# A graph layer kernel on one core: the product with W_r in a third gather stage, one stored row per node instead of two

## The chip, the core and the metric

The kernel runs on one core of one Trainium2 chip. A core has TensorE (PE, matrix products into PSUM), VectorE (DVE), ScalarE (ACT), GpSimd (POOL, which here issues the indirect DMAs) and SyncE (SP, which issues the plain DMAs); they run side by side and wait for each other by semaphores. The time is that of one execution on the device in microseconds (us), the median of several runs: 2688.31 us for the kernel before, from three runs between 2688.16 and 2688.74.

## The reference

There are 12500 nodes with 256 features (D) and 200000 edges, sorted by destination. With xn the normalised x, the reference computes

```python
agg = _mean_aggregate(xn, edge_index, N)           # mean of xn[src] over each node's incoming edges
gnn = relu(agg @ W_l.T + b_l + xn @ W_r.T) + xn
# mix: linear attention with 8 heads, then a two-layer MLP, each with a layer norm
Q, K = elu(xn @ Wq) + 1, elu(xn @ Wk) + 1
msg = _layernorm(attention(Q, K, xn @ Wv) @ Wm, g1, b1)
mix = xn + _layernorm(relu(concat([xn, msg]) @ W1) @ W2, g2, b2)
x = x + gnn + mix
# ffn: a router picks the 6249 tokens of largest weight
xf = _layernorm(x)
weights = xf @ wr + br
y = (gelu(xf[sel] @ w1 + b1) @ w2 + b2) * weights[sel]
x = x + xf + scatter(y)
```

## The kernel before

Nodes are padded to 98 blocks of 128 and are handled two blocks at a time, in 49 steps. After a first part that normalises x, writes it as a table `xtab` of node rows (two halves in 16 bits) and sorts out the edges' block numbers, come these stages:

- **Key steps** (49, `k_body`): keys, values and queries of two blocks; the transposed rows go to `xt_d`, the queries to `q_d`.
- **Message steps** (49, `m_body`): query times key sums, product with Wm, norm, the MLP with W1 (`m_hidden`) and W2 (`m_mlp_out`), one step late, norm; the result with the terms of xn goes to `r_d`.
- **Gathers**, beside both: the edges are cut in 392 groups of 512. GpSimd gathers four times 128 source rows per group (line 631) into a ring of six slots and waits for a free slot (`grp_used`). DVE makes a one-hot of the destinations for each block that a group touches (line 778), in a ring of four; TensorE adds the rows up with eight products of one-hot and rows (lines 1365 and 1367, function `seg`), and DVE adds the sum of a finished block into `agg` (line 788, `add_before`). A key step holds two groups, a message step six; in the code of TensorE and DVE each `seg` stands between the products of its step, and this written order is the order of the work.
- **Node steps** (49, `g_body`): ACT scales the sums to means (line 1243), TensorE transposes them (1350), ACT copies them back (1250), TensorE adds the products with W_r and W_l (1517), DVE adds b_l (963), applies relu and adds the row of `r_d` (966), takes the statistics of the norm (852 to 860); ACT writes the normalised row and the row of the result (1276), both of which SP stores to `ff_d` and, the second, to `out`; DVE takes the dot product with wr (950) for the token weight (955).
- **Choice of tokens**: eight rounds of counting (1003, PE 1535), then ranks and the list of chosen nodes.
- **Feed-forward steps** (25 of up to 256 tokens, `f_body`): GpSimd gathers rows of `ff_d` (line 654) and scatters results (664); TensorE makes each product of single-precision numbers from three of split halves (1576), 96 matmuls a step; ACT applies gelu, DVE makes the low halves (1085), the token weights and the results.

`steps(eng, body, n, unroll)` writes the first `unroll` steps out, puts the middle ones in a loop of `unroll` steps per pass, and writes the last out; where the number is Python's, code is straight.

Of the kernel before, what the change touches and what calls it, by code (L numbers as in the profile page):

```python
# [5 lines left out]
f32 = mybir.dt.float32  # L6
# [16 lines left out]
KG, MG = 2, 6  # L23
NG = NSUP * (KG + MG)
# [31 lines left out]
assert 0 < LASTC < P and KG * 3 == RING and MG == RING  # L56
# [43 lines left out]
def build(nc, x, src, dst, W_l, b_l, W_r, Wq, Wk, Wv, Wm, W1, W2, g1, b1, g2, b2, wr, br, w1, fb1, w2, fb2, out):  # L100
# [13 lines left out]
    with ctx:  # L114
# [12 lines left out]
        ff_d = nc.dram_tensor("ff_d", (NPAD, 2 * D), f32, kind="Internal").ap()  # L127
# [42 lines left out]
        fb2_s = sb("fb2_s", [P, D])  # L170
        wr_s = sb("wr_s", [P, D])
# [43 lines left out]
        G_T = (BA, BD)  # L215

# [6 lines left out]
        wts_in = sem("wts_in")  # L223
        wlr_in = sem("wlr_in")
# [75 lines left out]
        g_in = [sem(f"g_in{i}") for i in range(4)]  # L300
# [5 lines left out]
        g_v = sem("g_v")  # L306
        g_base = sem("g_base")
        g_w = sem("g_w")
        ff_out = [sem(f"ff_out{i}") for i in range(2)]
# [13 lines left out]
        f_xT_h = sem("f_xT_h")  # L323
        f_xT = sem("f_xT")
# [5 lines left out]
        f_w = sem("f_w")  # L330
# [36 lines left out]
        gxT = [w1_s[:, s, :].rearrange("p (a b) -> p a b", a=2) for s in range(4)]  # L367
        gma = [part(work, 2048 + 512 * s, (2, D)) for s in range(2)]
        gaT = [part(work, 3072 + 512 * s, (2, SB)) for s in range(2)]
        gx1 = [part(work, 4096 + 512 * s, (2, D)) for s in range(2)]  # L370
        gff = [part(work, 5120 + 1024 * s, (2, 2 * D)) for s in range(2)]
        gs = onehot[:, :, :, :].rearrange("p k t m -> p (k t m)").bitcast(f32)[:, 0:2 * D].rearrange("p (a b) -> p a b", a=2)
# [15 lines left out]
        s_blk = topk[:, 1200:1200 + NSEL]  # L388
# [6 lines left out]
        sel_idx = pool2[:, 1168:1168 + NSEL].bitcast(i32)  # L395
# [3 lines left out]
        fstg = [pool2[:, 1760 + 2 * k:1762 + 2 * k].bitcast(i32) for k in range(FSLOTS)]  # L399
# [31 lines left out]
        def m_place(i, t):  # L431

            g = KG * NSUP + t
            return g % RING, g // RING + i
# [10 lines left out]
                       (fb2_s[:, :], fb2.unsqueeze(0).to_broadcast([P, D])),  # L445
                       (wr_s[:, :], wr.rearrange("d o -> o d").to_broadcast([P, D])),
# [3 lines left out]
                       (fb1_s[:, :], fb1.rearrange("(c p) -> p c", p=P))]  # L450

# [8 lines left out]
        def _(e):  # L460
# [83 lines left out]
            for i in (NSUP - 2, NSUP - 1):  # L544
                e.wait_ge(m_r, i + 1)
                e.dma_start(rows(r_d, 2 * i), mr[i % 2]).then_inc(r_out[i % 2], 16)
            for s in range(2):
                e.wait_ge(r_out[s], 16 * len(range(s, NSUP, 2)))
# [1086 lines left out]
```

## Time and profile before

| | |
|---|---|
| median of three runs | 2688.31 us |
| profiled execution: time, span | 2688.11 us, 2686.4 us |
| PE busy | 2269.3 us (84%) |
| PE weight loads | 1880.8 us (70%) |
| DVE busy | 1324.9 us (49%) |
| ACT busy | 958.1 us (36%) |
| POOL busy | 1617.3 us (60%), of it line 631 1478.2 |
| granted TensorE clock, mean | 0.913 of full speed |
| chain that ended last | PE 35%, POOL 33% (line 631 32%), issue 14%, DVE 12% |
| DMA | 412.28 MB, mean 153 GB/s |

The span reaches from the first to the last instruction; the time also holds what lies around it, 1.7 us here. Busy shares are averages over stages with different limits, so they say little about a single stage. PE's matmuls overlap, so what a product costs is better read from the starts of neighbours. A row of the order of time gives the start and the duration in us, the engine, the line, the operation, what it writes and reads, and how many of a kind follow each other; in brackets the idle time ahead of it and what ended it.

### The profile page before, as it was taken

Reading aid. Unit: us, or ns where it says so; the run is one execution under the profiler, and the core shown is the slowest. Engines: PE = TensorE matmul, PEld = TensorE weight load, DVE = VectorE, ACT = ScalarE, POOL = GpSimd, SP = SyncE. Lnnn points to the kernel's source line nnn. Section 1 sums busy time; section 2 is a strip of 40 time slices with the busy share of each in tenths; the row PEclk is TensorE's granted clock in tenths of the full one; section 3 lists DMA queues with packets and bytes.
Section 4 is the critical chain, followed back from the end, with each engine's and each line's share of the span. In section 5 each row is a group of like instructions: output and inputs, shape, how many; then the busy total and the mean of one; then the engine's idle time right before and its main releaser. Section 6 shows DMA issues by size and latency. Waiting matters only on the chain.

```text
span 2686.4 us, 50791 instructions
## 1 busy us (share of the span) xinstructions
PE 2269.3 (84%) x13646; PEld 1880.8 (70%) x13647; DVE 1324.9 (49%) x3290; ACT 958.1 (36%) x2185; POOL 1617.3 (60%) x1719
## 2 busy tenths in 40 slices
PE   1299999988988898888888888888888999379998
PEld 1287777766776776676767776676766777269998
DVE  7644444443334334443444444545454788854444
ACT  7433333321222222222222222222222899235544
POOL 2577777777777777777777777777774000023332
PEclk7599999998888889989988999999999999579999
DMA  9766666664444444444444444444442899212221
GB/s 313 219 196 190 184 186 182 181 187 138 140 138 142 139 140 137 144 140 140 137 143 140 136 140 142 142 138 138 137 144 86 275 312 311 92 48 67 66 66 42
DMA packets 229947, 412.28 MB, mean 153 GB/s; under 512 B 38193, under 2 KB 129715, under 8 KB 229886
## 3 DMA queue, kind: packets, MB, share of 16 engines
q0 software_dynamic: 81296, 224.22, 29.2%
q1 hardware_dynamic: 147774, 186.59, 20.9%
q10 hardware_dynamic: 816, 0.79, 0.1%
q8 instruction: 22, 0.36, 0.1%
q14 instruction: 39, 0.32, 0.0%
HBM read 315.13 MB, written 96.32 MB: 153 GB/s over the span
## 4 chain that ended last, share of the span: by engine, by line
PE 35%; POOL 33%; issue 14%; DVE 12%; DMA 3%; ACT 1%; DVEq 1%; POOLq 0%
POOL gath_raw L631 32%; PE ps L1576 11%; PE ps L1410 5%; PE ps L1442 4%; PE ps L1365 4%; PE ps L1367 3%; DMA gath_raw<-xtab,srcI 2%; PE ps L1424 2%; DVE work L966 1%; DVE onehot L963 1%; PE ps L1452 1%; DVE onehot L950 1%; PE ps L1350 1%; PE ps L1484 1%; PE ps L1465 1%
## 5 line engine op out<-in xcount | busy, mean ns | idle before, releaser
L631 POOL DMA_INDIRECT gath_raw<-xtab,srcI x1563 | 1478.2, 946 | 476.4 <-issue 461.5
L1365 PE MATMUL ps<-gath_raw,onehot 128*128 128x256 f16 x1956 | 495.5, 289 | 197.8 <-DMA gath_raw<-xtab,srcI 106.7
L1367 PE MATMUL ps<-gath_raw,onehot 128*128 128x257 f16 x1956 | 497.7, 290 | 0.0
L778 DVE SCALAR_TENSOR_TENSOR onehot<-ps,blkbase,dstF 128x512 f32 x489 | 353.3, 746 | 262.2 <-issue 175.1
L1442 PE MATMUL ps<-work,w_s 128*128 128x256 f32 x1568 | 403.2, 415 | 0.7
L1365 PEld LDWEIGHTS ps<-gath_raw,onehot 128*128 x1956 | 199.7, 102 | 287.7 <-issue 254.0
L1442 PEld LDWEIGHTS ps<-work,w_s 128*128 128x128 f32 x1568 | 319.2, 209 | 49.5 <-issue 0.5
L852 DVE BATCH_NORM_STATS2 stats<-ps 128x6 f32<-128x256 f32 x196 | 74.4, 422 | 490.3 <-PE ps L1484 480.1
L1576 PE MATMUL ps<-split_raw 128*128 128x256 f32 x2376 | 292.7, 285 | 1.7 <-DVE split_raw L1076 1.5
L1576 PEld LDWEIGHTS ps<-split_raw 128*128 128x128 f32 x2376 | 287.8, 192 | 2.4 <-issue 1.9
L1193 ACT ACTIVATE work<-ps 128x512 f32<-128x512 f32 x98 | 58.5, 597 | 643.5 <-PE ps L1442 643.5
L1367 PEld LDWEIGHTS ps<-gath_raw,onehot 128*128 x1956 | 200.9, 103 | 43.7
L643 POOL COPY agg<-agg 128x2 int32 (+2 forms) x25 | 6.7, 268 | 347.3 <-DVE agg L1065 309.3
L1410 PE MATMUL ps<-wkv_s,work 128*128 128x256 f32 x784 | 183.8, 388 | 5.0 <-issue 4.2
L1452 PE MATMUL ps<-w_s,work 128*128 128x256 f32 x784 | 182.1, 385 | 1.0 <-ACT work L1193 0.7
L1410 PEld LDWEIGHTS ps<-wkv_s,work 128*128 128x128 f32 x784 | 146.6, 192 | 25.0 <-issue 4.8
L1452 PEld LDWEIGHTS ps<-w_s,work 128*128 128x128 f32 x784 | 145.0, 190 | 20.0 <-ACT work L1193 1.1
L1350 PE MATMUL ps<-ident,work 128*128 128x128 f32 x784 | 126.9, 285 | 16.1 <-ACT work L1243 15.7
L1310 ACT ACTIVATE agg<-ps,fb_s 128x256 f32<-128x256 f32 x200 | 83.9, 470 | 137.8 <-PE ps L1576 137.7
L664 POOL DMA_INDIRECT out_rows<-agg x49 | 48.5, 990 | 135.7 <-DVE agg L1105 123.7
L1198 ACT ACTIVATE small<-small 128x2 f32<-128x2 f32 x98 | 19.8, 203 | 303.4 <-DVE small L860 303.1
L1465 PE MATMUL ps<-kvbd,work 128*128 128x128 f32 x392 | 111.3, 379 | 14.5 <-issue 9.8
(204 smaller groups left out, 3157.4 us busy)
## 6 DMA issues: line engine op xcount, KB each, us to landing
work<-x_in SPq DMA_DIRECT2D x98, 256.0 KB, 3.7
ff_d<-work SPq DMA_DIRECT2D x49, 512.0 KB, 2.8
gath_raw<-xtab,srcI POOLq DMA_INDIRECT x1563
agg<-x_in SPq DMA_DIRECT2D x14, 896.0 KB, 7.2
xtab<-gath_raw SPq DMA_DIRECT2D x14, 896.0 KB, 4.9
xt_d<-work SPq DMA_DIRECT2D x49, 256.0 KB, 4.1
q_d<-work SPq DMA_DIRECT2D x49, 256.0 KB, 2.4
work<-q_d SPq DMA_DIRECT2D x49, 256.0 KB, 3.3
```

What stands on the lines that cost most here:

```text
L631: e.indirect_dma_start(out=gath[:, TPG * s + t, 0:2 * D], out_offset=None, in_=xtab[:, :], in_offset=bass.IndirectOffsetOnAxis(ap=srcI[:, ...
L778: v.scalar_tensor_tensor(out=onehots[:, ds(p % OHN * TPG, TPG), :], in0=ps[:, columns:columns + 1, 0:P].to_broadcast(shape), scalar=blkbas ...
L852: last = v.bn_stats(ln_st[k][:, u, :], src[:, u, :])
L1310: last = a.activation(fh[:, c, :], bank(BB + h)[:, c % 2, :], ACT.Gelu_apprx_tanh, bias=fb1_s[:, c:c + 1])
L1350: last = t.transpose(bank(b)[:, c, u * P:(u + 1) * P], of[:, u, c * P:(c + 1) * P], ident[:, :])
L1365: t.matmul(ps[:, ds(BG + k % 2, 1), 0:D], oh, gath[:, r, 0:D], start=False, stop=False, skip_group_check=True)
L1367: last = t.matmul(ps[:, ds(BG + k % 2, 1), 0:AGW], oh, gath[:, r, D:2 * D + 1], start=False, stop=q == TPG - 1, skip_group_check=True)
L1410: last = t.matmul(bank(BC + b)[:, u, :], kxT[s][:, c, u * P:(u + 1) * P], wkv_s[:, c, b * D:(b + 1) * D], start=c == 0, stop=c == 1)
L1442: last = t.matmul(bank(BD + h)[:, o_ % 2, :], w1_s[:, c, o_ * P:(o_ + 1) * P], (mxT[s] if c < 2 else mynT)[:, c % 2, :], start=c == 0, sto ...
L1452: last = t.matmul(bank(BF)[:, u, :], mh1[:, c, u * P:(u + 1) * P], w2_s[:, c, :], start=c == 0, stop=c == 3)
L1465: t.matmul(bank(BB)[:, u, c * P:(c + 1) * P], q, kvbd[:, c, :], start=True, stop=True)
L1576: last = t.matmul(to, left[l], right[r], start=start and k == 0, stop=stop and k == 2)
```

## The change

The 49 message steps hold five groups instead of six, and a third stage of 49 steps (`l_body`) follows them with one group each. In each of its steps TensorE multiplies the transposed rows of two blocks (loaded again from `xt_d`) with W_r, DVE adds b_l from PSUM to SBUF (`l_even`), and SP stores the 128x512 result to the new `lin_d`. The last message step's MLP products stand in the first two steps of that stage, with their norms on DVE. TensorE's message loop and the new one are written out six times per pass instead of two; each message step begins with a group, ahead of the query product. The ring of one-hots has six entries instead of four.

In the node steps TensorE reads the row of `lin_d` through the identity into PSUM (128x512) and adds the W_l products to it; DVE's one operation from PSUM applies relu and adds `r_d`. Means and variances of all blocks are kept; scale and shift are computed for two steps at a time on four columns. ACT writes only the row of the result. The token weight is computed at the end from the dot product of the row before the norm, its mean and its scale, for all 98 blocks at once. PSUM banks for the sums: four instead of two; buffers of sums: five instead of two; of loads and stores: four. The steps are straight code on all engines.

`ff_d` is gone. Four numbers per node (mean, a factor, the token weight; 16 bytes) go to `coef_d` from DVE's first search round (`coefficients`), and a feed-forward step gathers each token's row from `out` and its numbers from `coef_d`, four gathers instead of two; DVE makes the normalised row from them (`f_norm`, ahead of the transposes), and no longer takes the dot product there. The weight rows `wr_s` and `fb2_s` are loaded after the last group, into the room of the gather ring.

```diff
-KG, MG = 2, 6
-NG = NSUP * (KG + MG)
+KG, MG, LG = 2, 5, 1
+NG = NSUP * (KG + MG + LG)
-OHN = 4
+OHN = 6
+GRING, GXRING, GBANKS = 4, 5, 4
+GCOEF = 4
-        ff_d = nc.dram_tensor("ff_d", (NPAD, 2 * D), f32, kind="Internal").ap()
+        lin_d = nc.dram_tensor("lin_d", (NPAD, D), f32, kind="Internal").ap()
+        coef_d = nc.dram_tensor("coef_d", (NPAD, GCOEF), f32, kind="Internal").ap()
+        GP = (BB, BC, BE, BF)
+        fb2_s, wr_s = (gath_raw[:, 5632 + 256 * k:5632 + 256 * k + D] for k in range(2))
...
# SyncE (the stores of the last two message steps and the loads of the node steps move into l_io)
+            l_load(0, 0)
+            l_load(1, 1)
+            def l_io(i, s, j):
...
+                if isinstance(i, int) and i == NSUP - 3:
...
+                    for k in range(GRING):
+                        g_load(k)
+                if isinstance(i, int) and i == NSUP - 1:
+                    e.wait_ge(grp_used, NG)
...
+                            e.dma_start(to, of).then_inc(wts_g, 16)
+                e.wait_ge(l_ps, i + 1)
+                if not (isinstance(i, int) and i >= NSUP - 2):
+                    l_load(i + 2, s)
+                e.wait_ge(l_ev, i + 1)
+                e.dma_start(rows(lin_d, 2 * i), llin[s]).then_inc(l_out[s], 16)
+            steps(e, l_io, NSUP, 2, 3)
-                e.dma_start(rows(ff_d, 2 * i), gff[s]).then_inc(ff_out[s], 16)
-                e.dma_start(rows(out, 2 * i), gff[s][:, :, D:2 * D]).then_inc(ff_out[s], 16)
+                e.dma_start(rows(out, 2 * i), gbase[i % GRING]).then_inc(base_out[i % GRING], 16)
...
# GpSimd, feed-forward part
-                    e.indirect_dma_start(out=frow[s][:, u, :], out_offset=None, in_=ff_d[:, :],
-                                         in_offset=bass.IndirectOffsetOnAxis(ap=fstg[s][:, u:u + 1], axis=0)
+                    e.indirect_dma_start(out=frow[s][0:r, u, D:2 * D], out_offset=None, in_=out[:, :],
+                                         in_offset=bass.IndirectOffsetOnAxis(ap=fstg[s][0:r, u, 0:1], axis=0)
+                                         ).then_inc(f_in[s], 16)
+                    e.indirect_dma_start(out=fco[s][0:r, u, :], out_offset=None, in_=coef_d[:, :],
+                                         in_offset=bass.IndirectOffsetOnAxis(ap=fstg[s][0:r, u, 1:2], axis=0)
                                          ).then_inc(f_in[s], 16)
...
# VectorE, third stage and node steps
+            def l_even(i, s, j):
+                e.wait_ge(l_ps, i + 1)
+                if past(i, 2):
+                    e.wait_ge(l_out[s], 16 * j)
+                v.tensor_tensor(llin[s], bank(BB + s), bcast(bl_s[:, :], 2), ALU.add).then_inc(l_ev, 1)
+            def l_body(i, s, j):
+                g = (KG + MG) * NSUP + i
+                seg(g, BA, *seg_values(e, mybir.EngineType.DVE, g, 1)[0])
+                if past(i, 1):
+                    l_even(i - 1, 1 - s, j - 1 + s)
...
-                own.link(v.tensor_tensor(gs, bank(BB + s), bcast(bl_s[:, :], 2), ALU.add))
...
+            def g_sum(i):
+                x = gx1[i % GXRING]
...
+                v.scalar_tensor_tensor(out=x, in0=bank(GP[i % GBANKS]), scalar=0.0, in1=gr[i % GRING],
                                        op0=ALU.max, op1=ALU.add).then_inc(g_s, 1)
...
+            def g_scale(q):
+                b = slice(4 * q, min(4 * q + 4, NBLK))
+                own.link(v.tensor_scalar(gve[:, b], gmv[:, b, 1], LN_EPS, None, ALU.add))
+                v.reciprocal(grc[:, b], gve[:, b]).then_inc(g_v, 1)
+            def g_affine(q):
...
+            def g_dot(i):
+                for u in range(2):
+                    last = v.tensor_tensor_reduce(out=gjunk[:, u, :], in0=gx1[i % GXRING][:, u, :], in1=wr_s[:, :], scale=1.0,
...
+            for i in range(NSUP):
+                g_sum(i)
+                if i % 2 or i == NSUP - 1:
+                    g_scale(i // 2)
+                g_dot(i)
+                if i % 2 == 0 and i > 0:
+                    g_affine(i // 2 - 1)
+            g_affine(NSUP // 2)
+            own.link(v.tensor_scalar(gsum, gsum, -1.0, None, ALU.mult))
+            own.link(v.scalar_tensor_tensor(out=gdot, in0=gmv[:, :, 0], scalar=gsum, in1=gdot, op0=ALU.mult, op1=ALU.add))
+            own.link(v.tensor_tensor(gdot, gdot, gf, ALU.mult))
+            own.link(v.tensor_scalar(wtok[:, :], gdot, br_s[:, 0:1], None, ALU.add))
...
+            def f_norm(i, s, j):
+                n = 1 if isinstance(i, int) and i == FSTEPS - 1 else 2
+                e.wait_ge(f_in[s], 64 * j + 32 * n)
+                for u in range(n):
+                    last = v.tensor_scalar(frow[s][:, u, 0:D], frow[s][:, u, D:2 * D], fco[s][:, u, 0:1], fco[s][:, u, 1:2],
+                                           ALU.subtract, ALU.mult)
+                last.then_inc(f_ff, 1)
...
# TensorE
-            def m_body(i, s, j):
-
+            def m_body(i, s6, j6):
+                s, j = s6 % 2, j6 * (RING // 2) + s6 // 2
+                g0 = KG * NSUP + MG * i
+                spans = seg_values(e, mybir.EngineType.PE, g0, 1)
+                seg(*m_place(s6, j6, 0), *spans[0])
                 e.wait_ge(m_q_in[s], 16 * j + 16)
...
-                seg(*m_place(i, 5), *spans[5])
-            steps(e, m_body, NSUP, 2)
-            e.wait_ge(m_ynT, NSUP)
-            for h in range(2):
-                m_hidden(NSUP - 1, (NSUP - 1) % 2, (NSUP - 1) // 2, h)
-            m_mlp_out(NSUP - 1)
+            steps(e, m_body, NSUP, RING)
+            def l_body(i, s6, j6):
+                s, j = s6 % 2, j6 * (RING // 2) + s6 // 2
+                seg(*l_place(s6, j6), *seg_values(e, mybir.EngineType.PE, (KG + MG) * NSUP + i, 1)[0])
+                if isinstance(i, int) and i == 0:
+                    e.wait_ge(m_ynT, NSUP)
+                    for h in range(2):
+                        m_hidden(NSUP - 1, (NSUP - 1) % 2, (NSUP - 1) // 2, h)
+                if isinstance(i, int) and i == 1:
+                    m_mlp_out(NSUP - 1)
...
+                        last = t.matmul(bank(BB + s)[:, u, :], lxT[s][:, c, u * P:(u + 1) * P], wrT[:, c, :],
+                                        start=c == 0, stop=c == 1)
+                last.then_inc(l_ps, 1)
+            steps(e, l_body, NSUP, RING, 2)
...
+                t.matmul(flat(to), ident[:, :], flat(glin[i % GRING]), start=True, stop=False, skip_group_check=True)
+                e.wait_ge(g_aT, i + 1)
+                for u in range(2):
+                    for c in range(2):
+                        last = t.matmul(to[:, u, :], gaT[i % 2][:, c, u * P:(u + 1) * P], wlT[:, c, :],
+                                        start=False, stop=c == 1, skip_group_check=True)
```

The names on the left of an arrow are what is written, on the right what is read. TensorE, between the last group of rows and the first node steps, before; 1442 and 1452 are the MLP of the last message step, 1350 the transposes of the means:

```order
L1376 MATMUL ps<-gath_raw 1x1
L1442 MATMUL ps<-work,w_s 128x256 x16
L1452 MATMUL ps<-w_s,work 128x256 x8
L1350 MATMUL ps<-ident,work 128x128 x8
L1517 MATMUL ps<-wrT,w_s 128x256 x2
L1517 MATMUL ps<-wlT,work 128x256 x2
```

The same place now; 1609 is the product with W_r in the third stage, 1448 are the transposes, 1626 the copy through the identity, 1630 the products with W_l:

```order
L1474 MATMUL ps<-gath_raw 1x1
L1609 MATMUL ps<-wrT,wkv_s 128x256 x4
L1448 MATMUL ps<-ident,work 128x128 x8
L1626 MATMUL ps<-w_s,ident 128x512
L1630 MATMUL ps<-wlT,work 128x256 x4
L1448 MATMUL ps<-ident,work 128x128 x4
```

The 24 MLP products are gone from behind the last group, and a node step has four products and one copy where it had eight products (the two rows of 1517 stand twice in a step).

VectorE in one node step before (`small` and `mv` hold the norm's numbers, `wtok` the token weights):

```order
L963 TENSOR_TENSOR onehot<-ps,bl_s 128x512
L966 SCALAR_TENSOR_TENSOR work<-onehot,work 128x512
L852 BN_STATS stats<-ps 128x6 x2
L856 BN_AGGR mv<-stats 128x2 x2
L858 TENSOR_SCALAR small<-mv 128x2
L859 TENSOR_SCALAR small<-mv 128x2
L860 RECIPROCAL small<-small 128x2
L950 ISA onehot,small<-work,wr_s 128x256
L950 ISA small 128x1
L950 ISA onehot,small<-work,wr_s 128x256
L950 ISA small 128x1
L955 TENSOR_SCALAR wtok<-small,br_s 128x2
```

And now, a step of the kind that also does the scale of two steps; what is kept lies in `gath_raw`:

```order
L1013 SCALAR_TENSOR_TENSOR work<-ps,work 128x512
L1017 BN_STATS stats<-work 128x6 x2
L1020 BN_AGGR gath_raw<-stats 128x2 x2
L1026 TENSOR_SCALAR gath_raw<-gath_raw 128x4
L1027 RECIPROCAL gath_raw<-gath_raw 128x4
L1039 ISA gath_raw<-work,gath_raw 128x256
L1039 ISA gath_raw 128x1
L1039 ISA gath_raw<-work,gath_raw 128x256
L1039 ISA gath_raw 128x1
```

One operation of 512 columns is gone, and the small ones stand once for two steps.

GpSimd in the last step of a pass of the feed-forward loop, before and then now (`out_rows` is the result, `agg` names the buffers there):

```order
L643 COPY agg<-agg 128x2
L654 DMA agg<-ff_d,agg 128x512 x2
L664 DMA out_rows<-agg 12544x256 x2
L71 REGISTER_ALU
L71 COMPARE_AND_BRANCH
```

```order
L693 COPY agg<-agg 128x4
L705 DMA agg<-out_rows,agg 128x256
L708 DMA agg<-coef_d,agg 128x4
L705 DMA agg<-out_rows,agg 128x256
L708 DMA agg<-coef_d,agg 128x4
L718 DMA out_rows<-agg 12544x256 x2
L73 REGISTER_ALU
L73 COMPARE_AND_BRANCH
```

Two gathers per step are added between the copy of the indices and the scatters.

## Rows read from the trace of the kernel before

**Rows 1.** Line 631: durations in ns, first and last start; waits (us, times).
```profile
L631 POOL DMA_INDIRECT gath_raw<-xtab,srcI x1563: 942/946/1147, 101.8 to 2054.8; - x196
  PE ps L1376: 14.9, 49
```

**Rows 2.** Waits of TensorE, 630 to 2060 us: total us, times, longest.
```profile
PE ps L1365 <- DMA gath_raw<-xtab,srcI: 95.7, 57, 3.2
```

**Rows 3.** Order of time, TensorE, message steps: start us, us, instructions.
```profile
1350.14 0.39 PE L1365 MATMUL ps<-gath_raw,onehot 128*128 128x256 f16 x1 [2.81 <-DVE onehot L778]
...
1352.06 5.63 PE L1442 MATMUL ps<-work,w_s 128*128 128x256 f32 x16
...
1437.75 0.53 PE L1465 MATMUL ps<-kvbd,work 128*128 128x128 f32 x2
...
1464.29 0.28 PE L1365 MATMUL ps<-gath_raw,onehot 128*128 128x256 f16 x1 [1.83 <-DMA gath_raw<-xtab,srcI]
...
1465.42 0.78 PE L1465 MATMUL ps<-kvbd,work 128*128 128x128 f32 x2
```

**Rows 4.** Order of time, last gather to first node step, TensorE and DVE.
```profile
2063.31 7.17 PE L1442 MATMUL ps<-work,w_s 128*128 128x256 f32 x32
...
2080.71 0.42 DVE L788 TENSOR_TENSOR agg<-agg,ps  x1 [0.19 <-issue]
...
2083.30 0.77 DVE L924 RECIPROCAL rcnt<-rcnt 128x98 f32<-128x98 f32 x1
...
2084.13 0.06 DVE L932 MEMSET small<- 128x1 f32 x1
...
2092.09 0.69 DVE L963 TENSOR_TENSOR onehot<-ps,bl_s 128x512 f32<-128x512 f32 x1 [6.93 <-PE ps L1517]
```

**Rows 5.** Busy us in one stretch: PE, PEld, DVE, ACT, POOL, clock, DMA share, GB/s.
```profile
2090.00:2297.00 207.00, 196.59 (x966) 162.15 (x964) 178.41 (x677) 192.44 (x524) 0.00 (x0) 0.99 0.86 295
```

**Rows 6.** Order of time, DVE, one node step.
```profile
2180.68 0.69 DVE L966 SCALAR_TENSOR_TENSOR work<-onehot,work 128x512 f32<-128x512 f32 x1
2181.40 0.75 DVE L852 BATCH_NORM_STATS2 stats<-work 128x6 f32<-128x256 f32 x2
2182.31 0.25 DVE L856 BATCH_NORM_AGGREGATE mv<-stats 128x2 f32<-128x6 f32 x2 [0.15 <-DVE stats L852]
2182.59 0.17 DVE L858 TENSOR_SCALAR small<-mv 128x2 f32<-128x2 f32 x1
...
2182.98 0.42 DVE L950 CUSTOM_DVE_ANT_0 onehot<-work,wr_s 128x256 f32<-128x256 f32 x1
...
2183.91 0.23 DVE L955 TENSOR_SCALAR wtok<-small,br_s 128x2 f32 x1 [0.15 <-DVE small L950]
2184.05 0.68 DVE L963 TENSOR_TENSOR onehot<-ps,bl_s 128x512 f32<-128x512 f32 x1
```

**Rows 7.** Order of time, TensorE, the same node step.
```profile
2183.38 0.66 PE L1350 MATMUL ps<-ident,work 128*128 128x128 f32 x4 [0.38 <-ACT work L1243]
2183.87 1.03 PE L1517 MATMUL ps<-wrT,w_s 128*128 128x256 f32 x4
```

**Rows 8.** Order of time, DVE, last node step and last token weight.
```profile
2293.78 0.69 DVE L963 TENSOR_TENSOR onehot<-ps,bl_s 128x512 f32<-128x512 f32 x1
...
2300.66 0.23 DVE L955 TENSOR_SCALAR wtok<-small,br_s 128x2 f32<-128x2 f32 x1
```

**Rows 9.** Order of time, GpSimd and DVE, one feed-forward step.
```profile
2504.42 0.18 POOL L643 COPY agg<-agg 128x2 int32 x1 [1.69 <-DMA out_rows<-agg]
...
2507.00 0.97 POOL L654 DMA_INDIRECT agg<-ff_d,agg  x1 [0.30 <-issue]
...
2512.74 0.69 DVE L1085 TENSOR_TENSOR split_raw<-agg,split_raw 128x512 fp32r<-128x512 f32 x1 [1.21 <-ACT split_raw L1302]
...
2516.39 0.18 POOL L643 COPY agg<-agg 128x2 int32 x1 [1.71 <-DMA out_rows<-agg]
```

**Rows 10.** Line 654 (gathers of the feed-forward part), issue to landing.
```profile
DMA to landing us min/median/max: 3.3/3.5/5.2
```

More of the change, by code:

```diff
@@ L323, in build @@
         f_xT_h = sem("f_xT_h")
+        f_ff = sem("f_ff")
         f_xT = sem("f_xT")
@@ L577, in _ @@
+            for s in range(GRING):
+                e.wait_ge(base_out[s], 16 * len(range(s, NSUP, GRING)))
             for s in range(FSLOTS):
@@ L923, in _ @@
             own.link(v.tensor_scalar(rcnt[:, :], agg[:, :, D], 1.0, None, ALU.max))
-            own.link(v.reciprocal(rcnt[:, :], rcnt[:, :]))
-            for s in range(2):
-                e.wait_ge(r_out[s], 16 * len(range(s, NSUP, 2)))
-            own_g = base + 2
-            v.memset(small[:, 43:44], 0.0).then_inc(agg_done, 1)
+            v.reciprocal(rcnt[:, :], rcnt[:, :]).then_inc(agg_done, 1)
+            l_even(NSUP - 1, (NSUP - 1) % 2, (NSUP - 1) // 2)
+            e.wait_ge(wts_g, 16 * len(tail_loads))
+            v.tensor_reduce(gsum, wr_s[:, :], AX.X, ALU.add)
             for r in range(HALFD):
@@ new lines, in g_dot @@
+            def g_dot(i):
+                for u in range(2):
+                    last = v.tensor_tensor_reduce(out=gjunk[:, u, :], in0=gx1[i % GXRING][:, u, :], in1=wr_s[:, :], scale=1.0,
+                                                  scalar=0.0, op0=ALU.mult, op1=ALU.add,
+                                                  accum_out=gdot[:, 2 * i + u:2 * i + u + 1])
+                own.link(last)
+            own.at(base + 1)
+            for i in range(NSUP):
+                g_sum(i)
[4 more added lines that the diff above has]
+                    g_affine(i // 2 - 1)
@@ L993, in _, with coefficients @@
             v.tensor_copy(s_low, s_key)
+            def coefficients():
+                v.tensor_copy(gcoef[:, :, 0], gmv[:, :, 0])
+                v.tensor_copy(gcoef[:, :, 2], wtok[:, :])
+                own.link(v.reciprocal(gve, gg))
+                v.tensor_tensor(gcoef[:, :, 1], gf, gve, ALU.mult).then_inc(coef_set, 1)
             def search(keys, first):
@@ L1081, in f_body @@
                 n = 1 if isinstance(i, int) and i == FSTEPS - 1 else 2
+                if not (isinstance(i, int) and i == FSTEPS - 1):
+                    f_norm(i + 1, (s + 1) % FSLOTS, j + (s + 1) // FSLOTS)
                 for h in range(4):
@@ L1531, in _ @@
+            g_turn(0)
+            g_turn(1)
+            e.wait_ge(l_ev, NSUP)
+            g_linear(0)
+            for i in range(NSUP - 1):
+                if i + 2 < NSUP:
+                    g_turn(i + 2)
+                g_linear(i + 1)
+            e.wait_ge(s_tab_set, 1)
             for r in range(NDIG):
```

279 lines of the change are left out of this document (139 added, 140 removed).

## The prediction

> **What bounds the kernel now.** I read the engines' busy time by stretch first, then GpSimd's line for the row gathers, then TensorE's waits in the long middle stretch, then the seams in order of time. The gathers of node rows (line 631) run from 101.8 to 2054.8 us of the span, 1563 of them, so one per (2054.8 - 101.8) / 1562 = 1.250 us, and GpSimd waited for a free ring slot 49 times, 14.9 us in all, never over 0.3 us [rows 1]. So up to 2055 GpSimd sets the pace: a key step (2 groups of 4 gathers) takes 10 us, a message step (6 groups) 30.0 us. TensorE fills most of that time, but waits for it: 95.7 us for gathered rows between 630 and 2060 us [rows 2]. After 2055 no gather is left and four things follow: a seam until the neighbour means may start (the DVE memset of line 932 at 2084.13), 7.96 us until the first result of W_l and W_r is read (2092.09) [rows 4], the 49 node steps until 2300.9 [rows 8], where all engines are nearly full (PE 196.6, DVE 178.4, ACT 192.4 us of 207) [rows 5], the choice of tokens, and the feed-forward part until the end, one step per 11.97 us [rows 9].
>
> **The message stage with five groups.** GpSimd needs 20 x 1.250 = 25.0 us a step instead of 30.0. Does TensorE manage it? The step from 1437.75 to 1465.42 took 27.67 us, at full clock nearly throughout, and holds one wait for rows, of 1.83 us [rows 3]: 25.84 us of TensorE's own pace, its waits for one-hots included. A group with a single one-hot takes 1.13 us (1464.29 to 1465.42) [rows 3], and most have one, some two: 1.33 on average (489 for 392 groups are 1.25, with more at the end), so 1.13 + 0.33 x 1.0 = 1.5 us. That leaves 24.3 us with one group less, 0.7 under 25.0. The group now ahead of the query product moves within the step; the six one-hots can only shorten the waits on DVE. The number of one-hots per group grows slowly to the end, by 0.1, some 0.5 us a step. And TensorE may fall behind first: six slots are 30 us of gathers, a row set lands some 3.5 us after its issue, and it uses slots up to 6 us apart, so some 20 us of lag cost nothing. I take nothing lost. If a step took x us, the loss would be 49 (x - 25.0) - 20.
>
> The clock is the uncertain part. After an idle time of 2.81 us ahead of line 1365 at 1350.14 the granted clock was at its lower level (1.2 GHz) for part of the next stretch, and 16 rows of line 1442 took 5.63 us [rows 3], where 32 take 7.17 at 2.4 GHz [rows 4]. With 0.7 us of room a step such gaps become rarer, which favours the change. In the new third stage a step is one group (1.5 one-hots there, 1.6 us) and four W_r products in 8 rows at 0.22 (7.17 / 32), 1.8: 3.4 us of TensorE in 5.0 us of GpSimd: room, but a gap in every step. The Trainium skill ("TensorE: Matmul & The Clock Gate", HAM oscillation) speaks against such loops: work in short bursts between waits can start at the low clock every time. At 1.2 GHz such a step would be some 6.4 us (most of it doubled); that is rival D.
>
> **The third stage itself.** 49 x 8 rows of line 1517 (wrT) at 0.22 us, 86 us of TensorE, move out of the node steps into time that GpSimd fills; DVE's addition of b_l (line 963, 0.69 us) goes with them. Covered by the gathers: nothing. SP loads xT and stores one row set a step, 256 KB each, with two buffers, so each has 10 us, nearly three times the 3.5 of a row gather [rows 10]: nothing. If the cover went, each us over 5.0 in a step would cost 49 less the 20 of lag.
>
> **The seam at the end of the gathers.** Before: the last group is followed by 48 rows of lines 1442 and 1452 from 2063.31, then two normalisations; only then DVE adds the last two sums from 2080.71 and releases the means at 2084.13 [rows 4]. After: these products stand in the first two steps of the third stage. The last rows, issued at 2054.8, land 3.5 us later, if they do as in [rows 10], at 2058.3; a group takes 1.5 us, to 2059.8; DVE's two sums, maximum and reciprocal keep their 3.42 us and start some 0.5 later: 2063.7. Gain 20.4 us. The two weight rows loaded at this point (128 KB each) and the 4 x 512 KB of early loads are hidden unless they land after 2069; at worst they cost 3 us. Between release and first result fewer products stand (6 instead of 8 of 128x256): 6.5 instead of 7.96 us, gain 1.5 (0 to 3).
>
> **The node steps.** The 48 periods from 2092.09 [rows 4] to 2293.78 [rows 8] are 4.20 us each. DVE does its operations without a gap worth the name: line 966 0.72 us (2180.68 to 2181.40), statistics 0.91, aggregate 0.28, three small operations 0.39, dot products 0.93, the router's sum 0.14, line 963 0.72: 4.09 [rows 6]. After: 963 gone (0.72), the small ones gone (0.39), the sum gone (0.14): 2.84. Every second step gets four operations on four columns, at the 0.15 each that the small ones take: 0.3 a step. Sum 3.15. The steps are written out, so the loop pass that makes 4.20 of 4.09 goes too. The others: PE had 0.49 us of transposes (2183.38 to 2183.87) [rows 7] and eight products of two rows at 0.22; now four products and a copy through the identity of 512 columns, worth two: 0.49 + 6 x 0.44 = 3.1. ACT keeps pace with DVE at 192.4 of 207 us now [rows 5] and loses two of its four normalised writes and its four small operations a step. DMA moves 768 KB a step instead of 1280: 250 GB/s in 3.15 us, under the 295 of now [rows 5]. Gain 48 x (4.20 - 3.15) = 50.4 us; the bounds are 3.0 (57) and 3.6 (29), since PE and DVE are now within 0.1 us of each other and the new order has more hand-overs.
>
> The Trainium skill ("Runtime: NRT & Kernel Launch", Instruction fetch mechanics) says that instruction fetch runs ahead only in straight code and that a taken branch out of the fetched window stalls. The trace agrees in that the average is 4.20 where a step inside a pass has 4.09. By this rule TensorE's message loop, written out six times instead of two, stalls longer at its eight passes; the ring's lag covers it, and the sum is the same.
>
> **Between the steps and the end.** Before, 7.1 us from the last line 963 (2293.78) to the last token weight (line 955, 2300.66 + 0.23) [rows 8]. After: last sum, statistics, aggregate, scale, dots 3.15; two affine pairs 0.5; four chained operations on 98 columns 1.05: 4.7. Gain 2.4. The coefficients (four operations, one a reciprocal that took 0.77 us in line 924 [rows 4]) stand in a wait of 0.7 us of the first search round: loss 0.7. Two more index operations: 0.35. First feed-forward step: two more gathers ahead of it at 0.97 + 0.30 [rows 9], 2.5, and DVE's f_norm ahead of the transposes, two 256-wide operations, between 0.3 and 0.9 (line 966 does 512 columns in 0.69): 0.7. Loss 3.2. If the last coefficient gather, 16 B a row, lands early, it is 1 us less: the skill ("DMA: Bandwidth & Descriptors", Anatomy of one DMA) gives 2.0 us of fixed time for a small one; the gathers here land in 3.5 [rows 10], and the row decides.
>
> **Feed-forward steps.** TensorE's 96 products set the 11.97 us. GpSimd now issues four gathers behind its copy (2504.42), the last starting at 2507.00 + 2 x 1.27 = 2509.5 and landing 3.5 later [rows 10], 2513.0; DVE's f_norm waits there, ahead of line 1085, which started at 2512.74 [rows 9]. It ends at 2513.8, the first half 0.7 later at 2514.5; TensorE needs that half a step (6 us) after it starts at about 2510, so at 2516. Room 1.5 us: nothing lost.
>
> **Sum.** -20.4 - 1.5 - 50.4 - 2.4 + 0.7 + 0.35 + 3.2 = -70.45 us. The profiled execution: span 2686.4, time 2688.1, 0.2 under the median of 2688.3. 2688.3 - 70.4 = 2617.9 us, put at 2618.
>
> **Rivals.**
> A, node steps at 3.6 us instead of 3.15: PE, DVE and ACT hand over in turn with none waiting in reserve. For: PE at 3.1 is as long as DVE. Against: four PSUM banks and five buffers between them, where two held before without a DVE wait. +22: 2640. Chance 0.14.
> B, late gathers in the feed-forward part: they land over 1.5 us later and each step waits 0.5. For: four gathers on one queue. Against: the room above. 24 x 0.5 = +12: 2630. Chance 0.09.
> C, the message step at 26.2 us, because the low clock stays in it for 3 to 4 us: 49 x 1.2 - 20 = +39: 2657. For: the low clock after a wait [rows 3]. Against: fewer waits for rows. Chance 0.08.
> D, the third stage at the low clock, 6.4 us a step: 49 x 1.4 - 20 = +49: 2667. Against: at the low clock TensorE is never idle, which is when it was at 2.4 GHz. Chance 0.03.
> E, slower: the message steps do not get shorter than now, TensorE's chain (query product, ACT, transposes, DVE statistics, ACT, transposes, each waiting for the one before) needs 27.8 us with one group less to cover it: 49 x 2.8 - 20 = +117: 2735. From 26.9 us a step (49 x 1.9 - 20 = 73) the whole gain is gone. For: the step of 27.67 is among the shortest seen. Against: 1.83 of it was a wait for rows and one group goes. Chance 0.04.
> The forecast has 0.60, and 2 in 100 are for a gain that mishaps eat to within 0.2% (5.4 us), about what a measurement of this kernel can tell from no change.
>
> **Numbers.** Forecast 2618, its own range 2607 to 2630. To hold 8 in 10 the range takes in A and B: 2606 to 2648. Faster by over 0.2%: 0.60 + A to D = 0.94; within 0.02; slower 0.04.
>
> **What would show it.** Gathers from 101.8 to about 2055 with no slot wait over 1 us; the means released at 2064; DVE's new sum (128x512 from PSUM) every 3.15 us, 49 of them from about 2070 to 2222; the feed-forward step still 11.95 us. Wrong: waits of GpSimd for TensorE's group matmul (C, D, E), the DVE sum waiting for PE in the node steps (A), DVE waiting for coefficient gathers and TensorE behind it (B).

## The result, and the profile after

The changed kernel takes 2750.5 us (median of 4 runs, 2744.3 to 2753.9), the kernel before 2688.5 beside it: ratio 1.0228, interval 1.0216 to 1.0241. It is slower by 62 us, where the forecast was 70 faster. The profiled run has a span of 2749.9 us and a time of 2751.6.

The first group is line 680 of the changed kernel (the gathers, line 631 before), with durations in ns, first and last start, and its waits. The second is TensorE's waits from 630 to 2060 us.

```profile
L680 POOL DMA_INDIRECT gath_raw<-xtab,srcI x1563: 940/946/1151, 101.9 to 2193.6; - x196
...
  PE ps L1474: 164.1, 108
```

```profile
PE ps L1463 <- DVE onehot L832: 137.7, 43, 6.3
PE ps L1463 <- issue: 12.8, 14, 4.2
PE ps L1463 <- DVE ps L844: 10.0, 14, 0.9
PE ps L1463 <- DMA gath_raw<-xtab,srcI: 1.1, 1, 1.1
```

The gathers end 138.8 us later than before, and GpSimd waits 164 us for TensorE to free slots where it waited 15 [rows 1]. TensorE no longer waits for rows (1.1 us, 95.7 before [rows 2]) but for DVE's one-hots: 137.7 us in 43 waits. The message step takes 28.0 us, not 25.0 (the mean of 49 steps, read from the starts of line 1474, the last product of each group).

DVE from 1471 to 1485 us, order of time:

```profile
1473.26 0.75 DVE L832 SCALAR_TENSOR_TENSOR onehot<-ps,blkbase,dstF 128x512 f32 x1 [0.25 <-issue]
1482.24 1.41 DVE L832 SCALAR_TENSOR_TENSOR onehot<-ps,blkbase,dstF 128x512 f32 x2 [8.22 <-issue]
```

TensorE over the same time:

```profile
1476.88 0.66 PE L1448 MATMUL ps<-ident,work 128*128 128x128 f32 x4
1483.43 0.39 PE L1463 MATMUL ps<-gath_raw,onehot 128*128 128x256 f16 x1 [5.89 <-DVE onehot L832]
1483.61 0.42 PE L1465 MATMUL ps<-gath_raw,onehot 128*128 128x257 f16 x1
...
1492.89 0.27 PE L1465 MATMUL ps<-gath_raw,onehot 128*128 128x257 f16 x1
```

DVE stands idle for 8.22 us and waits for nobody ("issue"): between the last one-hot of one pass of its loop and the first of the next. TensorE has made its transposes, needs that one-hot for its next group, waits 5.89 us and then runs at the lower clock: the granted clock is at 1.2 GHz from 1480.8 to 1487.6 us, where the 128x257 product takes 0.42 us; nine us later it takes 0.27. The records of DVE's control instructions, which the views leave out, split the 8.22: from the loop's branch at 1473.98 to the next instruction at 1478.16 nothing at all happens (4.18 us), then the load of the step's 15 registers takes 3.42 (three per group, read from a table that says which blocks a group touches), the rest is register work. The same place in the kernel before, DVE again:

```profile
1430.09 0.43 DVE L790 TENSOR_SCALAR ps<-nought 128x257 f32 x1
1435.56 0.75 DVE L778 SCALAR_TENSOR_TENSOR onehot<-ps,blkbase,dstF 128x512 f32 x1 [5.04 <-issue]
```

There the load took 4.08 us (18 registers), but from branch to next instruction there are 0.32 us: no hole. In the message stage of the changed kernel this hole, a stretch behind the loop's branch in which DVE has no record at all, is there at 22 of 23 branches (the 23rd leaves the loop), 3.1 to 4.4 us each, 80 us in all; before at none. The page shows the same in its DMA queues of instructions, here of the changed kernel:

```profile
q8 instruction: 99, 1.62, 0.2%
q14 instruction: 155, 1.27, 0.1%
```

The kernel before has 22 and 39 packets in these rows:

```profile
q8 instruction: 22, 0.36, 0.1%
q14 instruction: 39, 0.32, 0.0%
```

The first number of such a row is the packets, the second their MB: so q14 fetches in packets of 8.2 KB and q8 in packets of 16.4 KB. In the message stage q14's packets come in bunches at DVE's branches (1473.7, 1475.3, 1475.6, 1478.8), and q8's one every 20 us or so.

The later stages did what the prediction says. The last group and the seam, and DVE's new sum (line 1013) from the first to the last step, and the end:

```profile
2204.78 0.16 PE L1474 MATMUL ps<-gath_raw 128*1 128x1 f16 x1
...
2206.24 1.99 PE L1609 MATMUL ps<-wrT,wkv_s 128*128 128x256 f32 x8 [1.29 <-DMA wkv_s<-xt_d]
```

```profile
2205.82 0.42 DVE L842 TENSOR_TENSOR agg<-agg,ps  x1 [1.39 <-PE ps L1474]
...
2208.40 0.77 DVE L991 RECIPROCAL rcnt<-rcnt 128x98 f32<-128x98 f32 x1
...
2216.01 0.69 DVE L1013 SCALAR_TENSOR_TENSOR work<-ps,work 128x512 f32<-128x512 f32 x1 [4.13 <-PE ps L1630]
...
2302.92 0.42 DVE L1039 CUSTOM_DVE_ANT_0 gath_raw<-work,gath_raw 128x256 f32<-128x256 f32 x1
...
2303.69 0.69 DVE L1013 SCALAR_TENSOR_TENSOR work<-ps,work 128x512 f32<-128x512 f32 x1
...
2306.82 0.69 DVE L1013 SCALAR_TENSOR_TENSOR work<-ps,work 128x512 f32<-128x512 f32 x1 [0.29 <-PE ps L1630]
...
2361.00 0.69 DVE L1013 SCALAR_TENSOR_TENSOR work<-ps,work 128x512 f32<-128x512 f32 x1
...
2365.00 0.27 DVE L1057 TENSOR_SCALAR wtok<-gath_raw,br_s 128x98 f32<-128x98 f32 x1
```

The stretch of node steps (busy us of PE, PEld, DVE, ACT, POOL; clock, DMA share, GB/s), beside [rows 5]:

```profile
2216.00:2361.00 145.00, 144.61 (x667) 109.15 (x665) 129.78 (x527) 113.09 (x253) 0.00 (x0) 1.00 0.77 243
```

49 sums from 2216.0 to 2361.0 are 3.02 us a step (4.20 before), alternately 2.92 and 3.13; TensorE is busy for 144.6 of the 145.0 us, and DVE waits for it 24 times, 11.2 us in all.

Span against span: gathers' end +138.8 (2054.8 to 2193.6); from there to the first node step 22.4 instead of 37.3, -14.9; node steps 145.0 instead of 201.7, -56.7; last sum to last token weight 4.3 instead of 7.1, -2.8; the rest 384.6 instead of 385.5, -0.9. Sum +63.5, which is 2749.9 - 2686.4.

### The profile page after: what moved, and what is told of

The parts are those of the page before. It is cut to its first block, busy times and chain, and to the rows that moved or that the text cites. A ratio compares the mean times of both kernels' runs of the same rounds, so it can differ in the third digit from the quotient of the medians.

```text
span 2749.9 us, 49999 instructions
## 1 busy us (share of the span) xinstructions
PE 2333.3 (85%) x13744; PEld 1931.6 (70%) x13745; DVE 1313.4 (48%) x3130; ACT 881.7 (32%) x1916; POOL 1663.5 (60%) x1768
## 4 chain that ended last, share of the span: by engine, by line
PE 58%; POOL 11%; issue 11%; DVE 9%; DVEq 7%; DMA 2%; ACT 1%; POOLq 0%
PE ps L1540 14%; POOL gath_raw L680 11%; PE ps L1689 10%; PE ps L1463 5%; DVEq L442 5%; PE ps L1465 5%; PE ps L1567 4%; PE ps L1583 3%; PE ps L1508 3%; PE ps L1630 3%; PE ps L1448 2%; DVE onehot L832 2%; DMA gath_raw<-xtab,srcI 2%; PE ps L1626 2%; PE ps L1569 1%
## 5 line engine op out<-in xcount | busy, mean ns | idle before, releaser
L1463 PE MATMUL ps<-gath_raw,onehot 128*128 128x256 f16 x1956 | 485.4, 285 | 231.6 <-DVE onehot L832 159.8
L1465 PE MATMUL ps<-gath_raw,onehot 128*128 128x257 f16 x1956 | 487.1, 285 | 0.0
L1463 PEld LDWEIGHTS ps<-gath_raw,onehot 128*128 x1956 | 196.5, 100 | 319.8 <-issue 287.1
L1540 PE MATMUL ps<-work,w_s 128*128 128x256 f32 x1568 | 418.0, 426 | 0.1
L1540 PEld LDWEIGHTS ps<-work,w_s 128*128 128x128 f32 x1568 | 331.0, 217 | 52.0
L1465 PEld LDWEIGHTS ps<-gath_raw,onehot 128*128 x1956 | 198.6, 102 | 45.6 <-issue 0.3
L693 POOL COPY agg<-agg 128x4 int32 (+2 forms) x25 | 6.7, 267 | 275.1 <-DVE agg L1155 235.8
L1567 PE MATMUL ps<-kvbd,work 128*128 128x128 f32 x392 | 130.3, 431 | 0.2 <-issue 0.2
L1335 ACT ACTIVATE work<-agg,rcnt 128x256 f32<-128x256 f32 x98 | 43.8, 498 | 220.1 <-DVE rcnt L991 220.1
```

Source lines behind the costliest of these rows:

```text
L1463: t.matmul(ps[:, ds(BG + k % 2, 1), 0:D], oh, gath[:, r, 0:D], start=False, stop=False, skip_group_check=True)
L1465: last = t.matmul(ps[:, ds(BG + k % 2, 1), 0:AGW], oh, gath[:, r, D:2 * D + 1], start=False, stop=q == TPG - 1, skip_group_check=True)
L1540: last = t.matmul(bank(BD + h)[:, o_ % 2, :], w1_s[:, c, o_ * P:(o_ + 1) * P], (mxT[s] if c < 2 else mynT)[:, c % 2, :], start=c == 0, sto ...
L1567: t.matmul(bank(BB)[:, u, c * P:(c + 1) * P], q, kvbd[:, c, :], start=True, stop=True)
```

## The experiments

Three theories stood at the start. **F:** DVE's message loop no longer lies where the fetched instructions can hold it, each pass fetches it anew, and the hole stands right ahead of the one-hot that TensorE's chain wants next. **O:** TensorE's new order (first group ahead of the query product) is the fault. **P:** its loop of six steps is. Places below are counted in the compiled list of DVE's instructions. Runs e1 to e4 were on one chip and f1 to f4 on another; the kernel before took 2689.1 and 2690.0 us there, 2688.5 beside the changed kernel, so times can be compared across them to 1 or 2 us. Ratios are against the kernel before on the same chip.

**e1, DVE's loop moved by 60 places.**

```diff
+            for _ in range(60):
+                alone(e, stood)
             e.wait_ge(k_acc, NSUP)
```

> The changed kernel with 60 one-semaphore instructions added on DVE ahead of its message loop, where DVE waits anyway (some 21 ns each, 1.3 us), so that the loop starts 60 places later in DVE's instruction list: places 1043 to 1359 instead of 983 to 1299, pages 4 and 5 of 256 instead of 3, 4 and 5. Theory F (the loop's branch back goes to a page no longer held, so DVE stalls 3.5 to 4.4 us in every second message step, and its first one-hot comes late for TensorE): the holes behind the loop branch (22 of them, 78.8 us) fall under 0.5 us each, instruction packets by the dozen go, the message step falls from 27.9 to 25.0 to 26.3 us, and the time to 2650 (2618 to 2685). Rival O (TensorE's order: its first group now stands ahead of the query product, and one group less covers the chain): the place in the list changes nothing, 2745 to 2752. Rival P (TensorE's loop of six steps refetches its code and lowers the clock): 2740 to 2752 too, since TensorE's list is the same.

Measured: 2642.8 us, ratio 0.9822 (0.9806 to 0.9839), 108 us faster than the changed kernel. The holes are gone (0.3 us at each branch), and so are two thirds of the packets (155 in the changed kernel, 39 before):

```profile
q14 instruction: 47, 0.38, 0.0%
```

TensorE's waits for one-hots fall from 137.7 us (the added lines shift the numbers, 1463 is 1465 here):

```profile
PE ps L1465 <- DVE onehot L832: 54.6, 33, 5.9
```

The message step is 26.0 us. 60 instructions that do nothing, at a place where DVE waits, take away most of the loss, with TensorE's program untouched: F, and neither O nor P alone.

**e2, the same by 140 places, and e3, the kernel before by 150.**

> The changed kernel with 140 such instructions (2.9 us): DVE's message loop lies in places 1123 to 1439, so still in two pages of 256, but in four half pages of 128, as in the changed kernel (in the first shift it is three). Theory F with pages of 256: as the shift by 60, within 5 us, no holes. Theory F with pages of 128 of which three are held for a loop: as the changed kernel, 2745 to 2755, holes of 3.5 to 4.4 us. Rivals O and P: 2745 to 2755.

> The kernel before with 150 such instructions (3.2 us) ahead of DVE's message loop: it lies in places 1181 to 1545, in three pages of 256 instead of two; nothing else differs. Theory F: the holes of 3.5 to 4.4 us behind the loop branch appear here too, 22 or 23 of them. What they cost depends on the cover: one group more stands there than in the changed kernel, the product of the queries comes ahead of the first group, and GpSimd's 30.0 us leave TensorE some 4 us a step: 2710 (2692 to 2750). Rivals O and P: holes or not, the time stays within 5 us of 2688.5, since DVE is half idle.

Measured: e2 2752.5 us (1.0244, 1.0221 to 1.0268), 22 holes of 3.2 us on average, step 27.9. It has more filling instructions than e1 and the full loss, so it is the place that counts and not the filling; and it isn't pages of 256 places. e3 2687.8 (0.9995, 0.9985 to 1.0004) and no hole, which missed its forecast. The expectations counted branches to the place right behind, which leave no record; without them the loop is 296 places long in the changed kernel, from 932, and 340 before, from 976. With one unknown constant between this count and the real places, 53 to 70, one rule fits all five: a loop that touches three blocks of 128 places has no hole, one that touches four has. The change shortened DVE's loop and made it worse: its two written-out steps are one group (22 places) shorter each, so the loop starts 44 places earlier and crosses one more border. The packets of 8.2 KB are a second sign of such blocks. No trace of the other kernels contradicts the rule: holes in e4, f2, g1, g2, g4, h1, h2; none in f1, f3, f4, g3.

**e4, only TensorE's order put back.**

```diff
-                spans = seg_values(e, mybir.EngineType.PE, g0, 1)
-                seg(*m_place(s6, j6, 0), *spans[0])
                 e.wait_ge(m_q_in[s], 16 * j + 16)
...
                 last.then_inc(m_nd_ps, 1)
+                spans = seg_values(e, mybir.EngineType.PE, g0, 1)
+                seg(*m_place(s6, j6, 0), *spans[0])
```

> The changed kernel with TensorE's order at the head of a message step as before: first the product of the queries, then the step's first group, then the hidden layer. DVE's loop keeps its three pages. Theory F: the holes stay (3.5 us, 22), the one-hot is wanted some 1.6 us later, the wait for it falls by that in every second step: 2710 (2690 to 2740). Rival O: this order was the fault, the message step falls to 25 to 26 us: 2620 to 2660. Rival P: 2740 to 2752.

Measured: 2625.4 us (0.9776, 0.9755 to 0.9797), step 25.4, 22 holes as in the changed kernel (3.5 us on average), q14 155 packets. O's forecast came in and F's (2710) missed; but O alone doesn't hold either, since e1 kept the order and gained 108 us. The gain here is 2.6 us a step. The product takes 2.1 us, so in every second step the one-hot is wanted that much later, 1.05 a step; and the stretches at the lower clock, which follow the waits, fall from some 6.5 to 2.5 us a step, worth at most another 2 us. Together that is enough; how the gain splits was not measured. With f1 below it makes a square: hole and order 2750.5, order alone 2642.8 (e1), hole alone 2625.4, neither 2612.3. Together they cost 138 us, singly 31 and 13.

**f1, both edits; f2, the loop cut elsewhere; f3, that and the order; f4, TensorE written out.** In f2 and f3 DVE's loop is turned: the branch and the register load stand ahead of its wait for line 1583, the operations keep their order. f2 also has 35 of the filling instructions ahead of the loop (not shown below), so that it touches four blocks and keeps its holes.

```diff
-            steps(e, m_body, NSUP, 2)
+            def m_turn(i, s, j):
+                spans = seg_values(e, mybir.EngineType.DVE, KG * NSUP + MG * i + 4, MG)
+                m_tail(i, spans[0])
+                m_head(i + 1, 1 - s, spans[1:])
+            m_head(0, 0, seg_values(e, mybir.EngineType.DVE, KG * NSUP, MG - 1))
+            steps(e, m_turn, NSUP - 1, 2)
+            m_tail(NSUP - 1, seg_values(e, mybir.EngineType.DVE, KG * NSUP + MG * NSUP - 1, 1)[0])
```

(`m_tail` is the wait, the norm and the last one-hot of a step, `m_head` the rest.)

> Both edits together once more, as on the chip where a gather took 1.53 us instead of 1.25 GpSimd covered everything. Theory F+O: 2612 (2605 to 2620). Rival O (behind the right order the hole is hidden): 2625 (2621 to 2630). If this chip too has gathers of 1.53 us: all kernels within 0.5% of each other, and nothing is told apart.

> DVE's message loop cut ahead of its wait for the product of line 1583, across four half pages, TensorE's order as in the changed kernel. Theory F with the place deciding: holes of 3 to 4 us there, yet a message step of 25.0 to 25.8 us, 2625 (2612 to 2645). Rival, that a refetch costs wherever it stands: 2735 to 2752. Rival O: 2735 to 2752.

> The same cut without the shift (three half pages, no holes) and with the product of the queries ahead of the first group. Theory F+O: 25.0 us a message step, 2610 (2603 to 2618), within 5 us of both edits. Rival O: 2625.

> Both edits, and TensorE's message stage written out for all 49 steps instead of a loop of six, so that its six stalls of 3.5 to 4.5 us at the branch back go; the packets of instructions stay. Theory F+O: hidden by the ring at 25.0 us a step, within 4 us of both edits. Rival P (TensorE's long loop is a part of the loss): 8 to 25 us below both edits.

Measured, with the message step: f1 2612.3 (0.9710, 0.9694 to 0.9727), 25.1; f2 2613.2 (0.9720, 0.9703 to 0.9736), 25.0; f3 2610.8 (0.9709, 0.9692 to 0.9725), 25.1; f4 2612.2 (0.9711, 0.9694 to 0.9727), 25.0. f2 is the cleanest: TensorE's order untouched, the same refetches as in the changed kernel, and 137 us gone. Its pages and DVE at one branch:

```profile
q14 instruction: 156, 1.27, 0.2%
```

```profile
1261.59 0.75 DVE L832 SCALAR_TENSOR_TENSOR onehot<-ps,blkbase,dstF 128x512 f32 x1 [0.70 <-issue]
1267.51 0.76 DVE L908 BATCH_NORM_STATS2 stats<-ps 128x6 f32<-128x256 f32 x2 [5.17 <-PE ps L1593]
```

```profile
L680 POOL DMA_INDIRECT gath_raw<-xtab,srcI x1563: 942/946/1151, 101.4 to 2054.2; - x196
```

The branch is at 1262.0 and its hole of 3.2 us lies in a wait of 5.17 for TensorE's line 1593 (1583 in the changed kernel). The gathers end at 2054.2, as forecast. f4 takes away TensorE's own stalls (in f1 3.4 to 4.5 us at six branches of its loop of 1530 places) and gains nothing, and f2 keeps them and loses nothing: P falls. What was left in e1 (31 us) stood where the register load still came ahead of the first one-hot and TensorE's first group ahead of the product: it goes when the load moves with the branch (f2) and also when only the order does (f1). That the load is this rest was not shown by itself (g3 below).

**e7, the kernel before with TensorE's loop written six times.**

> The kernel before with TensorE's message loop written out six times instead of two and nothing else. Rival P (TensorE's long loop costs in itself: a refetch of 3.4 to 4.3 us at each of some seven passes, and packets all along): the stalls appear; with 4 us a step of TensorE's room under GpSimd's 30.0 they cost nothing by theory F: 2689 (2685 to 2694). By rival P 7 x 4 = 28 us and more: 2705 to 2730.

Measured: 3147.2 against 3141.0 (1.0014, 0.9998 to 1.0031). On this chip a gather came every 1.53 us on average instead of 1.25. The median is still 1.25: 185 of the 1562 came more than 2 us after the one before, and the trace puts 291 us of GpSimd's idle time down to "remote", for which it shows no cause, and 176 us to TensorE (15 before). So this chip has waits of its own and the run says little. The kernels of f1 to f3 ran here first, as e5, e6 and e8: 3123.4, 3120.5 and 3117.2 us, ratios 0.9935, 0.9917 and 0.9926. So on such a chip the kernel with both edits is faster than the one before by 0.7%, not by 2.9%.

**g1 and g2, h1 and h2: the hole in the kernel before, and the order there.** g1 and h1 are the kernel before with 60 such instructions, four blocks; g2 and h2 have TensorE's first group ahead of the query product as well.

> The kernel before with 60 one-semaphore instructions ahead of DVE's message loop. By the five kernels seen so far, a loop on DVE that touches three blocks of 128 instructions has no hole and one of four has; this one touches four. Theory F: holes of 3 to 4.4 us behind the loop branch, 22 of them, but six groups and GpSimd's 30.0 us cover them: 2690 (2685 to 2700). Rival H (a hole costs in any order): 2720 to 2765.

> As the run beside, and TensorE's first group ahead of the product of the queries, as in the change; still six groups, no third stage. Theory F with the order as the part that lays the hole bare: TensorE's message step becomes 27.9 + 1.5 us for the sixth group = 29.4 on average, under GpSimd's 30.0 but with the hole in every second step only: 2695 to 2725. If the one group less is what lays it bare: 2690 (2685 to 2697).

> The kernel before with holes behind its loop branch, at gathers of 1.25 us if the chip gives them. Theory F: covered by six groups, the product of the queries ahead of the first group and GpSimd's 30.0 us: 2692 (2686 to 2702). Rival H (a hole costs in any order): 2720 to 2765.

> The same with TensorE's first group ahead of the product of the queries, still six groups. At gathers of 1.53 us this pair differed by 2.8%. Theory F with the order as the part that lays the hole bare: 2720 to 2770. If it takes the missing group too: 2690 to 2705.

Measured with gathers at 1.25 us: h1 2688.8 against 2688.9 (1.0001, 0.9992 to 1.0011), with 22 holes of 3.1 us; h2 2691.8 (1.0012, 1.0003 to 1.0022), though TensorE there waits 108.6 us for one-hots (39.9 before; line 1367 is 1365 before):

```profile
PE ps L1367 <- DVE onehot L778: 108.6, 26, 6.9
PE ps L1367 <- DMA gath_raw<-xtab,srcI: 46.2, 22, 4.9
```

The waits for rows fall by half in exchange, from 95.7 [rows 2]. With six groups GpSimd's 30.0 us cover both faults; with five its 25.0 don't. So the group less lays bare what hole and order do together: h1's forecast came in, and of h2's two it was the second, that the loss takes the missing group too. On a chip with late gathers like e7's (1.55 us on average in g1) g1 was 1.0014 (1.0000 to 1.0027) and g2 1.0295 (1.0263 to 1.0326). Why the order costs 3% there and 0.1% at 1.25 us was not found.

**g3, the register load split** (3 ahead of the first one-hot, 12 behind), **and g4, f2 with four one-hots.**

> The changed kernel shifted by 60 (no holes, 2642.8), with DVE's load of 15 registers split: three ahead of the step's first one-hot, twelve behind it. Theory L (what is left in the way of the first one-hot is this load, 3.4 us after the branch): the first one-hot comes 2 us and more earlier in each step, 2620 (2610 to 2630). Rival O (what is left is TensorE's order): 2638 to 2648.

> The kernel with the loop cut ahead of the wait (2613.2), with four one-hots in the ring instead of six. Theory F: DVE never runs six pairs ahead, since it waits for TensorE's product between them: 2613 (2608 to 2622). Rival R (the longer ring carries the message stage): 2630 and more.

Measured on that same chip: 1.0039 (1.0018 to 1.0059) and 0.9986 (0.9971 to 1.0002). With gathers at 1.59 us and more on average neither can be set beside e1 or f2: what the load alone costs and what the six one-hots are worth stay open.

## Why the prediction was wrong

**The message stage** is the step that failed: "I take nothing lost". The changed kernel lost 138.8 us there. That TensorE's own work fits under 25.0 us with one group less was sound: with the hole out of the way the step is 25.0 and the gathers end at 2054.2 for a forecast of 2055 (the 24.3 itself can't be seen behind GpSimd's pace). Two terms were put at nothing. One is DVE: the prediction took DVE's one-hots as part of "TensorE's own pace" and never asked what precedes the first one-hot of a step. The other is the order, "the group now ahead of the query product moves within the step": with the hole it cost 125 us (2750.5 to 2625.4), without it 31 (2642.8 to 2612.3). Half of the first could have been seen, though not the hole, which the kernel before doesn't have: there DVE sat idle 5.04 us at the end of a pass between two one-hots, and that was hidden by one group more behind the norm's wait and by the query product, both of which the change takes from there. From after the loss is 49 x (28.0 - 25.0) = 147, less some of the 20 of lag: 138.8.

**The refetch** was looked for on the wrong engine. The Trainium skill ("Runtime: NRT & Kernel Launch", Instruction fetch mechanics) says that a taken branch whose target has left the fetched window stalls for a DMA. The prediction used it for TensorE's loop of six, where the traces agree (3.4 to 4.5 us at its branches in f1) and the stall is hidden (f4). It fits DVE as well, whose loop looked only shorter. The prediction also read the rule into the node steps before, 4.20 us on average for 4.09 within a pass; that isn't borne out: DVE's branches there take 0.3 us each, and q14 brings two packets in the first 30 us of that stage's 200 and then none until its end. For most engines the Trainium skill gives, in the same section, a window of two blocks of 256 instructions; by it e2's loop, which with the constant lies between 1125 and 1438 and so in blocks 4 and 5, would have no hole. It had 22, and the measurement decides.

**Rival E** named the size (27.8 us a step, +117, for 28.0 measured) but put it on TensorE's own chain; with that chain untouched f2 runs at 25.0. C (low clock) was an effect: 6.5 us a step with the waits, 2.1 in f2, where only DVE's program differs. D did not come: the third stage took 4.8 us a step, at a granted clock of 0.96. A did not: 3.02 against 3.15, 6 us better. There TensorE sets the pace, with 3.02 for the 3.1 it was put at, and not DVE: its shorter steps come to 2.92, and in the longer ones, 3.13, it waits some 0.3 for TensorE. B did not: the small gathers land in 2.3 us (median), not 3.5. That is nearer the fixed 2.0 us that the Trainium skill ("DMA: Bandwidth & Descriptors", Anatomy of one DMA) gives. DVE waits for them 18.3 us in all, 6.0 of it once, and the step is 11.97 us still (line 693 at 2489.38 and 2501.35).

**The seam**: 15.4 us forecast from the last gather to the first node step, 20.3 in f2 (2054.2 to 2074.5); the last group came at 2063.2, not 2059.8, so TensorE was some 3 us behind. In the changed kernel it was 22.4. **The end**: 2.8 gained for 2.4; the search and feed-forward part 0.9 faster instead of 4.25 slower (line 693 still comes every 11.97 us; which of the small losses put there failed to come stays open, but for the small gathers).

With DVE's loop cut elsewhere and nothing else of the change touched (f2) the time is 2613 for the 2618 forecast. That nearness is partly luck: in f2's profiled run the seam was 4.9 us worse than forecast, the node steps 6.3 better and the part behind them 5.8 better.

## What to carry to other kernels

Where a group of work is taken from a step, ask for each engine what stands between its last operation of one pass and its first of the next, since that cover goes first; put the branch and the register loads of a loop ahead of a long wait, not ahead of what another engine wants next. Look at the page's rows of instruction packets in both kernels: a jump there (39 to 155) says that a loop is fetched anew at each pass, and an edit elsewhere in that engine's program can set it off. Whether it costs anything depends on what waits behind the branch: f2 has 156 such packets and is 137 us faster.

## What the runs showed of the hardware

On DVE a loop in three blocks of 128 instructions ran without refetch, and one in four blocks was fetched anew at each pass, whatever its length (296 places with and without holes, 340 too); at gathers of 1.25 us DVE stood still for 2.8 to 4.4 us each time. The blocks rest on one constant fitted to five kernels. TensorE's loop of 1530 places stalled at each of its six branches back, the one of 574 in the kernel before at none. In the message loops of the changed kernel and the one before the load of 15 registers took 1.6 or 3.4 us, of 18 registers 1.6 or 4.1. On two of the five chips of the experiments a gather came every 1.53 to 1.61 us on average instead of 1.25, at the same 0.95 us of GpSimd's own and the same median of 1.25, with waits for "remote" that the others don't show.
